# End of the attention's pair stage: last exponential ahead of the copy of the values, moves of the last two rounds issued from two queues

## The reference

```python
latent_kv = x @ w_kv_down
kv = latent_kv @ w_kv_up
k, v = (kv[..., :HD], kv[..., HD:])
q = (x @ w_q).reshape(Bx, Tx, N_HEAD, HEAD_SIZE)
att = jnp.einsum('bqhd,bkhd->bhqk', q, k) * scale
att = jnp.where(causal, att, -jnp.inf)
att = jax.nn.softmax(att, axis=-1)
y = jnp.einsum('bhqk,bkhd->bqhd', att, v)
return y.reshape(Bx, Tx, HD) @ w_out
```

## Time and profile before

| | |
|---|---|
| median of 3 runs | 1958.25 us (1957.36 to 1960.66) |
| the profiled execution's own time | 1958.33 us |
| its span, first to last instruction | 1957.1 us |
| mean granted TensorE clock | 0.971 |
| busy, share of the span | PE 92%, weight load 66%, DVE 65%, ACT 45%, POOL 35% |
| moves issued | 1152 (12 x 24 x 4) |
| DMA queue of SP | 173.72 MB, 36.8% of 16 engines |
| DMA queue of ACT | 6.30 MB, 1.1% of 16 engines |

### The profile page before, as it was taken

The page is one execution under the profiler, slowest core; times in us unless marked ns, Lnnn a source line. Parts: engine busy times, 40 slices in busy tenths (PEclk is TensorE's granted clock), DMA queues, the critical chain, the costliest instruction groups (busy, mean ns, idle before and its releaser), DMA issues.

```text
span 1957.1 us, 41278 instructions
## 1 busy us (share of the span) xinstructions
PE 1796.4 (92%) x16417; PEld 1282.2 (66%) x16417; DVE 1271.3 (65%) x2787; ACT 885.0 (45%) x1958; POOL 675.7 (35%) x1058
## 2 busy tenths in 40 slices
PE   7999998998999989899889998989989999889898
PEld 4766674667666667566756666756675666765667
DVE  4688846634788883753578887464467888656445
ACT  4567614222467662322256675322145666432223
POOL 2455531230155553123115555202312555420230
PEclk9899999999999999999999999989999999999999
DMA  8566640051266663004136556203115666520500
GB/s 221 124 154 157 142 145 1 2 86 34 74 151 146 144 139 116 1 18 70 34 99 152 142 140 146 91 1 62 26 34 134 147 146 140 116 87 2 87 1 23
DMA packets 128560, 182.65 MB, mean 93 GB/s; under 512 B 33296, under 2 KB 89328, under 8 KB 127344
## 3 DMA queue, kind: packets, MB, share of 16 engines
q1 hardware_dynamic: 114928, 173.72, 36.8%
q10 hardware_dynamic: 13440, 6.30, 1.1%
HBM read 62.44 MB, written 4.24 MB: 34 GB/s over the span
## 4 chain that ended last, share of the span: by engine, by line
PE 59%; DVE 14%; SPq 13%; ACT 7%; DMA 4%; issue 2%; POOL 0%; DVEq 0%
SPq L919 13%; PE scores L441 8%; PE bank L648 6%; PE scores L432 6%; PE scores L628 5%; PE bank L685 4%; DVE prob L749 4%; DMA placed<-prob 4%; PE bank L441 4%; PE bank L432 3%; PE scores L1557 2%; PE scores L1476 2%; ACT prob L849 2%; PE scores L1155 2%; DVE stats L282 2%
## 5 line engine op out<-in xcount | busy, mean ns | idle before, releaser
L648 PEld LDWEIGHTS bank<-placed,v_t 128*64 128x64 f32 x4608 | 255.7, 139 | 99.7 <-issue 99.7
L849 ACT ACTIVATE prob<-prob,neg_max 128x768 f32<-128x768 f32 (+5 forms) x384 | 273.7, 714 | 91.6 <-DVE neg_max L741 91.5
L648 PE MATMUL bank<-placed,v_t 128*64 128x128 f32 x4608 | 277.7, 277 | 37.8 <-DMA placed<-prob 29.6
L286 POOL TENSOR_TENSOR rstd<-rstd,minus_half 128x2 f32<-128x2 f32 x96 | 69.2, 720 | 660.3 <-DVE rstd L285 660.3
L628 PE MATMUL scores<-k_t,q_t 64*128 64x128 f32 (+10 forms) x2176 | 289.4, 412 | 0.0
L749 DVE STREAM_TRANSPOSE prob<-prob 128x1536 f32<-128x1536 f32 x128 | 226.0, 1774 | 35.5 <-ACT prob L849 34.8
L811 POOL COPY placed<-prob 32x768 f32<-32x768 f32 x256 | 210.2, 821 | 19.9 <-issue 0.4
L628 PEld LDWEIGHTS scores<-k_t,q_t 64*128 64x128 f32 x2176 | 166.1, 188 | 71.9 <-issue 60.5
L741 DVE CUSTOM_DVE_ANT_1 prob<-scores,hx 128x128 f32<-128x128 f32 (+4 forms) x320 | 165.4, 576 | 54.4 <-PE scores L628 30.4
L798 POOL COPY rec_wide<-rec 128x128 f32<-128x128 f32 x256 | 65.0, 289 | 338.2 <-DVE rec L753 241.1
L849 ACT ACTIVATE hx<-hx,neg_max 128x896 f32<-128x896 f32 (+1 forms) x128 | 119.6, 934 | 76.5 <-DVE neg_max L741 75.7
(11 more groups left out here) (242 smaller groups left out, 3385.7 us busy)
## 6 DMA issues: line engine op xcount, KB each, us to landing
placed<-prob SPq DMA_DIRECT2D x768, 96.0 KB, 2.2
placed<-hx SPq DMA_DIRECT2D x384, 96.0 KB, 2.1
f<-in_L_ffn_f SPq DMA_DIRECT2D x16, 2048.0 KB, 12.9
x<-in_L_attn_x SPq DMA_DIRECT2D x8, 512.0 KB, 4.4
mod_rows<-mod_scratch SPq DMA_DIRECT2D x32, 128.0 KB, 5.6
out<-x SPq DMA_DIRECT2D x16, 256.0 KB, 2.1
w_ring<-in_L_attn_w_q ACTq DMA_DIRECT2D x24, 128.0 KB, 3.0
w_ring<-in_L_attn_w_kv_up ACTq DMA_DIRECT2D x48, 64.0 KB, 2.1
```

The lines of the kernel that those rows point to most:

```text
L286: step = pool.do(lambda e, ts=ts: nc.gpsimd.tensor_tensor(rstd[:, ts], rstd[:, ts], minus_half[:, ts], op=ALU.pow), var, filled)
L648: last = nc.tensor.matmul(out_bank[rows_, at_:at_ + P], v_t[pair % 2][:, j, rows_], placed[m % 2][:, :, head, first_block(m, i) + j, :], s ...
L849: nc.scalar.activation(p_, p_, ACT.Exp, scale=-1.0, bias=neg_max[:, k:k + 1], accum_out=row_sum[:, k:k + 1]).then_inc(flow["exp_done"], 1)
```

## The change

Three edits. In the last three rounds ACT does its last exponential ahead of the copy of the values of round m - 2. Of the twelve moves of round 22 SP issues the first eight and ACT the last four, of round 23 SP the first six and ACT the last six; ACT's moves of round 22 stand in round 23, behind its last exponential and ahead of the copy of round 21's values, and its moves of round 23 stand behind the loop, ahead of the copy of round 22's values. The order of the late tiles is written out as a tuple.

```diff
@@ -523,6 +523,7 @@
         MOVES = [(src, dst) for dst in range(GROUPS) for src in range(GROUPS) if src != dst]
+        ACT_MOVES = {ROUNDS - 2: MOVES[8:], ROUNDS - 1: MOVES[6:]}
@@ -868,6 +869,14 @@
+            def move(m):
+                e.wait_ge(flow["shuffled"], base["shuffled"] + HEADS * (m + 1))
+                e.wait_ge(flow["values_done"], base["values_done"] + m - 1)
+                for source, target in ACT_MOVES[m]:
+                    e.dma_start(placed[m % 2][target * GROUP:(target + 1) * GROUP, source, :, :, :],
+                                prob[m % 3][source * GROUP:(source + 1) * GROUP, target, :, :, :]
+                                ).then_inc(flow[MOVED[m % 2]], 16)
@@ -888,9 +897,13 @@
                 exponential(m, large, 0)
-                if m > 1:
+                if m > 1 and first:
                     read_values(m - 2)
                 exponential(m, large, 1)
+                if m == ROUNDS - 1:
+                    move(m - 1)
+                if m > 1 and not first:
+                    read_values(m - 2)
                 if first:
                     job(*first)
@@ -899,6 +912,7 @@
                 if m > 0:
                     copy_rec(m - 1)
+            move(ROUNDS - 1)
             read_values(ROUNDS - 2)
             copy_rec(ROUNDS - 1)
             read_values(ROUNDS - 1)
@@ -915,7 +929,7 @@
-                for source, target in MOVES:
+                for source, target in MOVES[:len(MOVES) - len(ACT_MOVES.get(m, ()))]:
                     e.dma_start(placed[m % 2][target * GROUP:(target + 1) * GROUP, source, :, :, :],
@@ -1356,7 +1370,7 @@
-        late = sorted(tiles_of(1), key=lambda t: OUT_ROUND[t])
+        late = (TH + 1, TH + 3, TH, TH + 2)
```

## The result

The changed kernel takes 1965.65 us (median of 20 runs, 1960.04 to 1970.33), the kernel before 1957.46 beside it (20 runs, 1949.84 to 1961.38). The ratio is 1.0042 with a 95% interval of 1.0031 to 1.0053, some 8.2 us. Forecast were 1960.1 and a range up to 1965.0.

The account below looks back on a forecast made before the run. The prediction took the chain to tile 0's head output (round 21's moves, values, ACT's copy, POOL's product) as the bound. On 1958.33 us, -0.65 + 1.6 + 0.8 = +1.75 gave 1960.1 us, range 1955.0 to 1965.0.

Parts of the forecast that it names:

- What bounds the stage: Pair stage, last three rounds: it ends earlier only if tile 0's head output starts earlier; round 23's moves are 3.9 us early.
- The new tuple: Order of the late tiles: worth nothing, since the old sort already gives the tuple's order for PE, DVE and POOL.
- the six moves of round 23: Issued on ACT behind the copies of round 21's values and the reciprocals: cover 5 us, cost 0.
- The -0.65 us of the second batch: Exponential no longer ahead of a 0.80 us transpose wait, so SP starts round 21 earlier: -0.65 us, at worst 0.
- The four moves of round 22 on ACT: Ahead of the copy of round 21's values, 0.50 us each: +1.6 first batch, +0.8 third, 0 second and fourth.
- rival 3: Second and fourth batch: values of round 21 and head output return to full clock, 6.7 us less, 1953.4 us; chance 0.13.
- The clock: Third batch's head output: gap grows from 2.04 to 2.8; if the clock falls, 1.7 more, 1961.8 us; chance 0.20.
- The first rival: ACT's and SP's queues wait for each other when issuing moves, delaying the copy: +8.2 us, 1966.5 us; chance 0.13.

Follow-up runs that it names:

- The run with the moves alone: Moves split between queues as in the changed kernel, but the copy ahead of the last exponential in all rounds, as in the kernel before; ratio 1.0006 to that kernel.

## Why the prediction was wrong, point by point

**What bounds the stage** was read rightly: only the chain to the head output of tile 0 counts, the moves of 22 and 23 are early anyway. The runs bear it out from both sides: splitting 22 and 23 behind the copy gave nothing, splitting 20 and 21 gave 0.32%.

**The new tuple** and **the six moves of round 23**: nothing, as forecast.

**The -0.65 us of the second batch** did not come, a second and smaller term that failed. It hung on a hand-over of that one execution: in the trace after, SP was in its string from round 20 (ended 720.16) to round 21 (720.25) with no wait for the transposes. The run with the moves alone has the old order and its SP goes from round 20 to 21 within 0.23 us (714.28 to 714.51), so it was a property of a trace, not of the kernel.

**The four moves of round 22 on ACT** is the step that failed. The mechanism was right, the term of +2.4 us was less than half of what came. It has three parts: one price too low, and twice a wait counted as cover that was not there.
- The price of an issue was taken as 0.50, the middle between 0.37 and 0.64. It is 0.62 and 0.03 between two. The lower end was the length of an issue of weights with nothing right ahead of it; right behind a move the same issue takes 0.596, and a move right behind another at least 0.609 on ACT. Four took 2.55 us, not 2.0: first batch +2.2 instead of +1.6 (5.03 against 2.85).
- The third batch was to lose 0.8, since its values of 21 had waited for SP and so ended only just in time. In both traces of the changed kernel they came straight behind the scores, the values of 20 having run in part at 1.2 GHz (4.51, mean granted clock 0.62 of full in both). The batch then loses as much as the first and more, +2.8 in the trace after. The cover that I had counted was a wait that is not there in every execution.
- The second and fourth batch were to lose nothing, with 1.8 us of slack. They lose 0.3 each in one trace and 0.3 and 0.9 in the other. The issues start with the last exponential, at 731.20, and the values were over at 733.42, 2.2 us later, less than the 2.55 that four issues take. In the trace of before some 4.3 us lay between the two, since those values were slowed (4.51) and had waited longer (3.08). So the same clock that gave back 1.67 us at these values (rival 3) also took away the cover.

Sum of the part: 5.6 and 6.1 us in the two traces, against 2.4.

**The clock** was kept as a case for the third batch alone. Head outputs of the changed kernel took 3.69 to 6.38, and all four with a gap over 4 ahead took 6.01 to 6.38, where no head output of the trace of before is over 5.38. So the clock adds 0.6 to 1.0 on top of the old 1.7 there. What is left between 5.6 to 6.1 and the 8.2 us of the medians is of that size. That split is not shown, only consistent, and the gap alone does not set the length: 6.66 and 6.75 came in other runs behind gaps of 2.93 and 2.87, and with eight issues ahead 5.27 behind one of 7.05.

**The first rival** named 1966.5, close to what came, for a reason that does not hold. ACT's issues take 0.617 in the median beside SP's, SP's 0.594 beside ACT's, and in the first batch ACT's last took 0.612 with SP already done (at 252.86). One queue standing in line for the other is not seen here. By the rule of the Trainium skill (Perfetto Trace Analysis, DMA Instruction — HWDGE (DVE, Sync)), that the issuing sequencers lock a shared descriptor generator for each DMA, it should have been; in these runs the lengths do not agree with it. (SP's issues of up to 1.99 us, which the prediction read as a sign for this rival, are 1.986 at most for the moves written as prob; the row it cites has only the other line, with 1.835. Both are from the trace of before, where ACT issues no moves.) The number agreed, the mechanism did not; **rival 3** did happen in the profiled execution (6.7 us regained in the second and fourth batch) without being an effect of the change.

The range stopped at 1965.0 and left larger losses to the first rival, because the case beyond it was tied to the lock and not to the plain sum at the upper bounds: 0.64 an issue, all four batches exposed, two of them with the clock's share. Four issues at 0.64 less the 0.4 that the sum for the first batch took off are 2.2 us a batch, so 8.8 in four, and that should have been inside.

## What to carry to other kernels

- Work for a second queue goes behind the instruction that others wait for, and only to what somebody waits for. Here the same issues cost 0.4% ahead of one copy and nothing behind it, and the split won only in rounds 20 and 21, whose landing PE waits for.
- An issue of such a move on ACT takes 0.6 us from all that follows it in the program, even though the arithmetic ahead of it goes on; only what fits beneath that arithmetic (here two issues under an exponential) is free.
- When a cover is itself a wait (values late because SP is late), price the step once with the cover and once without, and let the range reach to the sum without it.

## What the runs showed of the hardware that was not expected

- The length of an issue depends on what the queue has just done: 0.334 us for a weight transfer on ACT by itself and 0.596 in the median where it follows moves; the moves of the changed kernel on ACT took 0.52 to 0.60 after a pause and 0.61 or more right behind another; SP's have 0.507 for the shortest and 0.593 in the median.
- Issues of two queues beside each other do not lengthen each other, but their data land later. After the change a move issued from ACT beside SP lands 2.8 us after the start of its issue in the median, one of SP beside ACT 2.7, and SP's others 2.2. With eight issues ahead, where 27 of ACT's run with nothing of SP beside them, those land in 2.2 too.
- Two executions of one program differ in which steps of PE are granted 1.2 GHz: with gaps of 2.04 to 2.34 us ahead, the same 48 or 16 matmuls took 2.84 or 4.51 and 3.69 or 5.38.
